# Attention weights of a graph layer: ScalarE bends seven of ten source tiles, VectorE multiplies them in one operation

## The chip, the core and the metric

The kernel runs on one core of a Trainium2 chip. The metric is the device time of one execution in microseconds (us); the core has TensorE (PE), VectorE (DVE), ScalarE (ACT), GpSimd (POOL) and the DMA queues, which run side by side and wait for each other through semaphores.

## What is computed

Two graph layers over 1250 nodes of 128 features and 20000 edges, each with a layer norm ahead of it and a residual sum behind it. The change lies in the first, an attention layer:

```
Wh = h @ W.T + b_W
s_s = Wh @ a_src
s_d = Wh @ a_dst
e = leaky_relu(s_s[src] + s_d[dst] + a_b[0], 0.2)
m = segment_max(e, dst);  ex = exp(e - m[dst])
denom = segment_sum(ex, dst)
h_prime = segment_sum((ex / denom[dst])[:, None] * Wh[src], dst)
```

A gated cell turns `h_prime` and `h` into new node states. The second layer does four steps of message passing by edge type, each with such a cell.

## The kernel before

The nodes are cut into ten tiles of 128. The attention isn't computed edge by edge. For each tile n of ten destination tiles the kernel counts how many edges run from each source node to each node of the tile, which gives ten blocks of 128 x 128 (one for each source tile i, source nodes on partitions). The weight of a block is this count times a function of the two scores, and because a leaky ReLU is the larger of two lines, that function is a product of exponentials up to one maximum: `max(fall[d], s_tall[s])`, where `fall` depends on the destination alone (a row, the same on all partitions) and `s_tall` on the source alone (a column). A further factor of the source, `s_gain`, is multiplied into `Wh` once. The matrix product of the weight blocks and `Wh` (with a column of ones for the denominator) then gives the attention sum of the tile.

The work of the ten tiles runs in turns J = 0 to 9, written out by hand for each engine (the functions `turn`), and staggered over them:

- VectorE in turn J makes the one-hot tiles of the turn's first half window (`one_hots`, into a ring of eight), unpacks the digits of tile J - 1 (`read_digits`), makes the weights of tile J - 2 (`weigh`), makes the one-hot tiles of the second half window, and takes the reciprocal of the denominator of tile J - 2 (`reciprocals`; that of tile 0 comes in turn 3 ahead of the digits).
- TensorE multiplies one-hot tiles (`window`, line 1441), turns the counts of tile J - 1 around into the other PSUM tensor (`count_turn`, line 1455), aggregates tile J - 2 with its weights (`aggregate`, line 1478), and multiplies the one-hot tiles of the second half.
- ScalarE evacuates the second half window of the turn before (`evac`, line 542), shifts the cell numbers of a coming window (`window_cells`, line 547), copies the attention row of tile J - 3 with its reciprocal (`attn_out`, line 582), evacuates the first half window, and brings the counts of tile J - 1 to SBUF (`counts_out`, line 554) and sums their excess (`excesses`, line 560). After turn 9 the calls for the last tiles are written out one by one, mixed with the first gates of the cell.

`weigh` is ten operations on VectorE per tile, line 965. It waits for the counts and, two tiles back, for the aggregation that frees its buffer; the weights go to two buffers in turn. The semaphore `probs` tells TensorE that they are done, and tells ScalarE that the counts may be overwritten.

Of the kernel before, what the change touches and what calls it, by code (L numbers as in the profile page):

```python
# [42 lines left out]
HOTS_BEFORE = (0, *accumulate(TILES))  # L43
AHEAD = 63
CELL_SETS = 4
SLOW = 5
LANE_PART = 20
WIN = 64
# [43 lines left out]
def build(nc, x, src, dst, attr, W, b_W, a_src, a_dst, a_b, res_W, res_b, Wi, Wh_g, bi, bh,  # L92
          W_edge, b_edge, W_ih, W_hh, b_ih, b_hh, out):
    with ExitStack() as ctx:
        def sb(name, shape, dt):
            return ctx.enter_context(nc.sbuf_tensor(name, shape, dt))
# [30 lines left out]
        def carve(shape, dt, size):  # L127
# [4 lines left out]
            if dt != BF16:  # L132
# [76 lines left out]
        s_peak = sb("s_peak", [P, 1], F32)  # L209
        s_back = sb("s_back", [P, 1], F32)  # L210
        s_tall = sb("s_tall", [P, NT], F32)
        s_low = sb("s_low", [P, 1], F32)
        s_flat = exp_b
        ab_col = sb("ab_col", [P, 1], F32)
# [68 lines left out]
                  "w_T w_sb bias_sb hn stats var rstd norm lanes "  # L283
                  "h_T h_sb b_cols proj_ps proj folded Wh_ps Wh s_ps s_rows d_ps s_dst s_peak s_up bent fallen s_fall s_gain gained")
        E1 = sems("e_", "sq link bound scale bias wide w_T w_sb spread rows_ps rows")
        K = sems("k_", "cellw pair slot evac digits countT absent counted excess rowmax logit "
                 "lmax shift exps probs probT probsb agg denom recip attn")
        G = sems("g_", "a_ps aS gates rz z uu vv n dd ee h turn")
        T = sems("t_", "ps full hi lo")
# [73 lines left out]
        def weights(n):  # L363
            return exp_b if isinstance(n, int) and n % 2 else exp_a
# [48 lines left out]
        def _(pool):  # L413
# [11 lines left out]
            g.iota(iota[:], pattern=[[1, CELLS]], base=0, channel_multiplier=0, **kw).then_inc(C.iota, 1)  # L425
            g.memset(zero16[:], 0.0).then_inc(C.const, 1)
            g.memset(power[:], -0.5).then_inc(C.const, 1)
            g.memset(few[:], 1.0 - BASE).then_inc(C.const, 1)
            g.memset(ones[:], 1.0).then_inc(C.const, 1)
            g.memset(Wh[:, :, P:P + 1], 1.0).then_inc(C.const, 1)  # L430
            for n, run in groupby(range(NS), lambda w: TILES[w]):
# [73 lines left out]
        def _(act):  # L505
# [74 lines left out]
            def attn_out(n, J):  # L580
                act.wait_ge(K.recip, n + 1)
                a.activation(attn[:, bass.ds(J, 1)].rearrange("p a d -> p (a d)"), psD[:, 0:P], ACT.Copy,
                             scale=denom_r[:, 0:1]).then_inc(K.attn, 1)

            def turn(J):
                if there(J - 1):
                    evac(J - 1, 1)
                    if 2 * J + 3 < NW:
                        window_cells(2 * J + 3)
                if there(J - 3):  # L590
                    attn_out(J - 3, J - 3)
                if J == 1:
                    falls()
                if there(J):
                    evac(J, 0)
                if 2 * J + 4 < NW:
                    window_cells(2 * J + 4)
                if there(J - 1):
                    counts_out(J - 1, count_sum[:, J - 1:J])
                    excesses(J - 1)  # L600

            def falls():
                act.wait_ge(S0.s_fall, 1)
                act.wait_ge(S0.d_ps, 1)
                a.activation(fall[:], smallf[:, 0:NP], ACT.Relu, bias=s_back[:, 0:1], scale=RISE).then_inc(S0.bent, 1)
                a.activation(s_tall[:], s_up[:], ACT.Exp, scale=RISE / SLOPE)
                act.wait_ge(S0.bent, 1)
                a.activation(fall[:], fall[:], ACT.Exp, scale=-1.0).then_inc(S0.fallen, 1)

# [46 lines left out]
            act.wait_ge(S0.s_ps, 1)  # L656
            a.activation(s_rows[:], smallf[:, 0:NP], ACT.Identity, bias=proj[:, 2:3]).then_inc(S0.s_rows, 1)
            turn(1)
            a.activation(s_gain[:], s_up[:], ACT.Exp).then_inc(S0.s_gain, 1)
            act.wait_ge(S0.s_gain, 1)  # L660
            for i in range(NT):
                last = a.activation(Wh[:, i], Wh[:, i], ACT.Copy, scale=s_gain[:, i:i + 1])
# [59 lines left out]


            evac(NT - 1, 1)
            attn_out(NT - 3, NT - 3)
            attention_in(0, 0)
            counts_out(NT - 1, count_sum[:, NT - 1:NT])
            attn_out(NT - 2, NT - 2)
            first_gates(0)
            excesses(NT - 1)  # L730
# [70 lines left out]
            with act.If(flag):  # L801
                act.sem_inc(K.probsb, NT)
                act.wait_ge(Z.weights, 1)
                a.activation(s_gain[:], s_up[:], ACT.Exp, scale=-1.0).then_inc(S0.s_gain, 1)
                act.wait_ge(S0.s_gain, 2)
                for i in range(NT):
                    last = a.activation(Wh[:, i], Wh[:, i], ACT.Copy, scale=s_gain[:, i:i + 1])
                last.then_inc(Z.plain, 1)
                a.activation(s_flat[:], s_rows[:], ACT.Copy, scale=SLOPE).then_inc(Z.flat, 1)
                with act.Fori(0, NT) as J:  # L810
                    slow_counts(J)
                    slow_absences(J)
                    counts_out(NT + J)
                    slow_exponentials(J)
                    probs_out(NT + J)
                    attn_out(NT + J, J)
                for c in range(NCH):
                    attention_in(NCH + c, c)
                    cell_gates(0, NCH + c, (NCH + c) % 2, c, CH)
                    cell_new(NCH + c, (NCH + c) % 2, CH)  # L820
                    second_norm(NCH + c, c)
                    second_h(NCH + c, c)
                with act.Fori(0, STEPS, 2) as s:
                    slow_step(s, 0)
                    slow_step(s + 1, 1)
# [6 lines left out]
        def _(dve):  # L832
# [125 lines left out]
            def weigh(n):  # L958
                dve.wait_ge(K.counted, n + 1)
                if n == 0:  # L960
                    dve.wait_ge(S0.fallen, 1)
                if n >= 2:
                    dve.wait_ge(K.agg, n - 1)
                for i in range(NT):
                    last = v.scalar_tensor_tensor(weights(n)[:, i * P:(i + 1) * P], fall[:, n * P:(n + 1) * P],  # L965
                                                  s_tall[:, i:i + 1], count[:, i * P:(i + 1) * P], ALU.max, ALU.mult)
                last.then_inc(K.probs, 1)

            def slow_row_max(J):
# [917 lines left out]
```

## Time and profile before

| what | us |
|---|---|
| median of 3 runs | 435.61 |
| lowest and highest | 435.06 and 438.87 |
| the profiled execution, its own time | 434.47 |
| its span, from the first to the last instruction | 432.3 |
| busy in the span: TensorE, VectorE, ScalarE, GpSimd | 370.1, 266.6, 150.8, 99.1 |

The span is what the trace covers, and the execution's own time has 2.17 us around it. Busy times of the engines overlap each other, so they don't add up to the span; an engine that is busy for a small part can still end the waits of another.

### The profile page before, as it was taken

To read this page: it belongs to the slowest core of one execution; us is meant where nothing else is said; L and a number is where in the kernel's file an instruction comes from. 1 tells how busy PE (TensorE), PEld (TensorE's weight loads), DVE (VectorE), ACT (ScalarE), POOL (GpSimd) and SP (SyncE) were. 2 spreads that over 40 slices of the span, in tenths; PEclk is the share of its full clock that TensorE was granted. 3 is DMA by queue.
4 is the path that set the end of the run, shared out by engine and by line. 5 is a ranking of instruction groups with operands and counts; after the bars stand their busy time and mean duration, and the time that the engine had idled before them with its cause. 6 is when DMAs were issued, how large, how long until landed. Compare 5 with 4: busy or idle time off the path is not lost.

```text
span 432.3 us, 6617 instructions
## 1 busy us (share of the span) xinstructions
PE 370.1 (86%) x2057; PEld 246.9 (57%) x2057; DVE 266.6 (62%) x797; ACT 150.8 (35%) x333; POOL 99.1 (23%) x136
## 2 busy tenths in 40 slices
PE   1459876777798888889899999999999999999993
PEld 0446543555556667644375674656655675747793
DVE  6997887688889765777365454436434545444144
ACT  3452266444445554443122222213122322312022
POOL 3102000000000000100177700577202775007300
PEclk9959996999999999999999999999999999999998
DMA  5200000000000000012213320233202242111200
GB/s 145 69 1 2 1 2 1 2 1 2 1 2 2 2 1 2 0 69 80 103 51 106 94 80 24 80 97 105 97 2 85 55 147 75 42 73 48 57 14 23
DMA packets 14498, 19.88 MB, mean 46 GB/s; under 512 B 2591, under 2 KB 7728, under 8 KB 14460
## 3 DMA queue, kind: packets, MB, share of 16 engines
q1 hardware_dynamic: 10276, 12.90, 8.4%
q0 software_dynamic: 2912, 5.97, 5.5%
q10 hardware_dynamic: 1272, 0.54, 0.5%
q8 instruction: 19, 0.31, 0.3%
q14 instruction: 19, 0.16, 0.1%
HBM read 8.27 MB, written 11.13 MB: 45 GB/s over the span
## 4 chain that ended last, share of the span: by engine, by line
PE 67%; DVE 19%; ACT 5%; issue 5%; DVEq 2%; DMA 0%; POOL 0%; SPq 0%; ACTq 0%; POOLq 0%
PE small L1590 27%; PE big L1572 7%; PE small L1478 6%; DVE scores L965 4%; DVE cell_hot L946 4%; PE big L1441 4%; PE small L1455 2%; PE small L1611 2%; DVEq L946 2%; PE small L1624 2%; PE big L1535 1%; PE small L1535 1%; PE small L1526 1%; PE small L1537 1%; PE small L1528 1%
## 5 line engine op out<-in xcount | busy, mean ns | idle before, releaser
L1590 PE MATMUL small<-nibbles,store 128*128 128x384 fp8e4 (+1 forms) x640 | 125.8, 353 | 1.3 <-DVE store L1118 0.8
L480 POOL DMA_INDIRECT scores<-messages,w_gat x91 | 87.7, 964 | 120.4 <-DMA messages<-store 93.9
L1590 PEld LDWEIGHTS small<-nibbles,store 128*128 128x128 f16 x640 | 62.3, 98 | 64.3 <-issue 7.2
L946 DVE TENSOR_SCALAR cell_hot<-iota,cell_w,fields 128x320 bf16<-128x320 f16 x231 | 65.7, 359 | 16.6 <-PE big L1441 15.6
L1441 PE MATMUL big<-cell_hot,store 128*128 128x320 bf16 x231 | 46.5, 324 | 14.0 <-DVE cell_hot L946 9.0
L721 ACT CAST store<-digit_words 128x512 f16<-128x512 f32 x40 | 24.6, 618 | 81.5 <-DVE digit_words L1114 81.5
L1114 DVE TENSOR_TENSOR digit_words<-big,edge_rows 128x512 f32<-128x512 f32 x40 | 27.4, 690 | 40.0 <-PE big L1572 39.9
L1441 PEld LDWEIGHTS big<-cell_hot,store 128*128 x231 | 31.3, 144 | 27.9 <-issue 25.6
L1572 PE MATMUL big<-wT,h 128*128 128x512 f32 x80 | 38.6, 599 | 2.3 <-ACT h L717 2.3
L1057 DVE SCALAR_TENSOR_TENSOR cell_hot<-rz,cell_hot 128x256 f32<-128x256 f32 (+2 forms) x29 | 11.0, 380 | 36.2 <-ACT cell_hot L692 36.2
L466 POOL TENSOR_TENSOR rstd<-var_e,power 128x2 f32<-128x2 f32 x5 | 3.5, 694 | 128.8 <-DVE var_e L1102 128.8
L1118 DVE TENSOR_TENSOR store<-digit_words,store 128x512 f16<-128x512 f32 x40 | 27.5, 689 | 6.1 <-ACT store L721 4.8
L691 ACT ACTIVATE rz<-small,gb 128x192 f32<-128x192 f32 (+1 forms) x14 | 6.2, 444 | 67.6 <-PE small L1537 67.6
L1455 PE MATMUL small<-nibbles,ident 128*128 128x512 fp8e4 (+1 forms) x120 | 25.3, 364 | 2.4 <-DVE nibbles L955 2.4
L965 DVE SCALAR_TENSOR_TENSOR scores<-scores,s_tall,tallies 128x128 f32<-128x128 f32 x100 | 27.2, 348 | 0.0
L1478 PE MATMUL small<-Wh,scores 128*128 128x129 f32 x200 | 24.8, 278 | 2.4 <-DVE scores L965 1.7
L1478 PEld LDWEIGHTS small<-Wh,scores 128*128 128x128 f32 x200 | 23.2, 191 | 5.1 <-DVE scores L965 3.4
L542 ACT CAST digit_words<-big 128x640 uint16<-128x640 f32 x20 | 13.8, 692 | 33.3 <-PE big L1441 18.1
L1230 DVE TENSOR_SCALAR aS<-small,edge_down 128x192 f32<-128x192 f32 (+2 forms) x24 | 9.7, 430 | 22.2 <-PE small L1590 17.3
L1572 PEld LDWEIGHTS big<-wT,h 128*128 128x128 f32 x80 | 14.5, 190 | 15.4 <-issue 10.6
L1455 PEld LDWEIGHTS small<-nibbles,ident 128*128 128x128 f16 x120 | 11.6, 102 | 15.8 <-DVE nibbles L955 4.5
L554 ACT ACTIVATE tallies<-small 128x1280 f32<-128x1280 f32 x10 | 12.4, 1238 | 19.9 <-DVE scores L965 10.7
(262 smaller groups left out, 493.2 us busy)
## 6 DMA issues: line engine op xcount, KB each, us to landing
messages<-store SPq DMA_DIRECT2D x40, 256.0 KB, 2.0
scores<-messages,w_gat POOLq DMA_INDIRECT x91, 2.5
xn<-in_x SPq DMA_DIRECT2D x1, 576.0 KB
out<-xn SPq DMA_DIRECT2D x4, 128.0 KB
store<-in_edge_attr SPq DMA_DIRECT2D x1, 256.0 KB
wn<-in_L_gnn_W_edge SPq DMA_DIRECT2D x1, 256.0 KB, 6.4
wn<-in_L_gnn_Wi ACTq DMA_DIRECT2D x1, 192.0 KB, 3.9
wn<-in_L_gnn_Wh_g ACTq DMA_DIRECT2D x1, 192.0 KB, 6.1
```

Source lines behind the costliest of these rows:

```text
L480: g.indirect_dma_start(out=rows16[:, u].rearrange("p a f -> p (a f)"), out_offset=None, in_=table_rows[s % 2][:], in_offset=bass.IndirectO ...
L542: a.copy(o.rearrange("p i (b d) -> p b i d", b=2), big[:, 2 * half:2 * half + 2, 0:HALF].rearrange("p b (i d) -> p b i d", d=SUB)).then_in ...
L721: a.copy(m16[s % 2][:, i, :, 0], full[:, i % 2].rearrange("p (t o) -> p t o", t=TYPES)).then_inc(T.hi, 1)
L946: last = v.tensor_scalar(half_hot[:, (before + q) % RING], iota[:, b * HALF:(b + 1) * HALF], cell_w[:, j % CELL_SETS, bass.ds(tile, 1)], f ...
L965: last = v.scalar_tensor_tensor(weights(n)[:, i * P:(i + 1) * P], fall[:, n * P:(n + 1) * P], s_tall[:, i:i + 1], count[:, i * P:(i + 1) * ...
L1114: v.tensor_tensor(full[:, i % 2], big[:, i % 2], edge_rows[:], ALU.add).then_inc(T.full, 1)
L1118: v.tensor_tensor(m16[s % 2][:, i, :, 1], full[:, i % 2].rearrange("p (t o) -> p t o", t=TYPES), m16[s % 2][:, i, :, 0], ALU.subtract).the ...
L1441: last = mm(big[:, 2 * half + b, 0:HALF], lane_hot[:, :, bass.ds(tile, 1)].rearrange("p l a -> p (l a)"), half_hot[:, (before + q) % RING] ...
L1455: last = mm(smallf[:, lo:hi], ident16[:], A8[:, q // 2, lo // P:hi // P, n * P:(n + 1) * P, q % 2], start=(q == 0), stop=(q == TYPES - 1), ...
L1478: last = mm(psD[:, 0:P + 1], w[:, i * P:(i + 1) * P], Wh[:, i], start=(i == 0), stop=(i == NT - 1), skip_group_check=True)
L1572: mm(big[:, i % 2], h1[:, i * P:(i + 1) * P], wT[:, W_EDGE:NWT].rearrange("p t o -> p (t o)"), start=True, stop=True).then_inc(T.ps, 1)
L1590: last = mm(bank[:, 0:w], m16[s % 2][:, i, t, part], A8[:, t % 2, i, lo:lo + w, t // 2], start=(i == 0 and part == 0 and t == 0), stop=(i ...
```

## The change

For source tiles 0 to 6 (`RAISED = 7`) the maximum goes to ScalarE. It holds the inverse of `s_tall` there and computes `raised = relu(fall * (1 / s_tall) - 1)`, one operation for each source tile, with a column of -1 as bias and the column of `s_tall` as scale. VectorE then makes the seven blocks with one operation 896 columns wide, `(raised + 1) * count`. The factor `s_tall` that was divided out is put into `s_gain` of these tiles, so both exponentials are now computed in two parts, 7 columns and 3. Source tiles 7 to 9 keep their three operations, which now come first. `raised` is one buffer, in memory that held the transposed weights of the other path, so ScalarE waits for the weights of the tile before until it overwrites it. GpSimd sets the column of -1 at the start. The core of the diff (left out are the declarations, the split of `s_gain` on the path that isn't taken here, and context):

```
+            def raises(n):
+                act.wait_ge(S0.fallen, 1)
+                if n >= 1:
+                    act.wait_ge(K.probs, n)
+                for i in range(RAISED):
+                    last = a.activation(raised[:, i * P:(i + 1) * P], fall[:, n * P:(n + 1) * P], ACT.Relu,
+                                        bias=below_one[:, 0:1], scale=s_tall[:, i:i + 1])
+                last.then_inc(K.raised, 1)
...
                 if there(J - 3):
                     attn_out(J - 3, J - 3)
+                if there(J - 2):
+                    raises(J - 2)
...
-                a.activation(s_tall[:], s_up[:], ACT.Exp, scale=RISE / SLOPE)
+                a.activation(s_tall[:, 0:RAISED], s_up[:, 0:RAISED], ACT.Exp, scale=-RISE / SLOPE)
+                a.activation(s_tall[:, RAISED:], s_up[:, RAISED:], ACT.Exp, scale=RISE / SLOPE)
...
-            a.activation(s_gain[:], s_up[:], ACT.Exp).then_inc(S0.s_gain, 1)
+            a.activation(s_gain[:, 0:RAISED], s_up[:, 0:RAISED], ACT.Exp, scale=1.0 / SLOPE)
+            a.activation(s_gain[:, RAISED:], s_up[:, RAISED:], ACT.Exp).then_inc(S0.s_gain, 1)
...
             evac(NT - 1, 1)
+            raises(NT - 2)
             attn_out(NT - 3, NT - 3)
             attention_in(0, 0)
             counts_out(NT - 1, count_sum[:, NT - 1:NT])
+            raises(NT - 1)
             attn_out(NT - 2, NT - 2)
...
-                for i in range(NT):
-                    last = v.scalar_tensor_tensor(weights(n)[:, i * P:(i + 1) * P], fall[:, n * P:(n + 1) * P],
-                                                  s_tall[:, i:i + 1], count[:, i * P:(i + 1) * P], ALU.max, ALU.mult)
+                for i in range(RAISED, NT):
+                    v.scalar_tensor_tensor(weights(n)[:, i * P:(i + 1) * P], fall[:, n * P:(n + 1) * P],
+                                           s_tall[:, i:i + 1], count[:, i * P:(i + 1) * P], ALU.max, ALU.mult)
+                dve.wait_ge(K.raised, n + 1)
+                last = v.scalar_tensor_tensor(weights(n)[:, 0:RAISED * P], raised[:, 0:RAISED * P], 1.0,
+                                              count[:, 0:RAISED * P], ALU.add, ALU.mult)
                 last.then_inc(K.probs, 1)
```

On ScalarE a middle turn (turn 5, say) read like this before, from the evacuation of the second half window of the turn before to the excesses; `digit_words` are the packed counts, `tallies` holds the counts and their excess:

```order
L542 CAST digit_words<-big 128x2x10x32 [waits k_digits,k_slot]
L547 ACTIVATE cell_w<-fields 128x160
L582 ACTIVATE attn<-small,denom_r 128x128 [waits k_recip]
L542 CAST digit_words<-big 128x2x10x32 [waits k_digits,k_slot]
L547 ACTIVATE cell_w<-fields 128x160
L554 ACTIVATE tallies,count_sum<-small 128x1280 [waits k_probs,k_countT]
L560 ACTIVATE tallies,excess_sum<-tallies,few 128x1280 [waits k_excess,k_counted]
```

In the changed kernel, whose line numbers are a little higher, the same turn reads so (`scores` is `fall`, and `raised` lies in `tallies`):

```order
L546 CAST digit_words<-big 128x2x10x32 [waits k_digits,k_slot]
L551 ACTIVATE cell_w<-fields 128x160
L586 ACTIVATE attn<-small,denom_r 128x128 [waits k_recip]
L594 ACTIVATE tallies<-scores,below_one,s_tall 128x128 [waits k_probs,s0_fallen]
L594 ACTIVATE tallies<-scores,below_one,s_tall 128x128 x6
L546 CAST digit_words<-big 128x2x10x32 [waits k_digits,k_slot]
L551 ACTIVATE cell_w<-fields 128x160
L558 ACTIVATE tallies,count_sum<-small 128x1280 [waits k_probs,k_countT]
L564 ACTIVATE tallies,excess_sum<-tallies,few 128x1280 [waits k_excess,k_counted]
```

Seven operations now stand between the attention copy and the evacuation of the first half window. On VectorE, the same turn before, from the unpacking of the digits to the first one-hot tile of the second half window:

```order
L954 TENSOR_SCALAR nibbles<-digit_words 128x10x128 [waits k_evac]
L955 TENSOR_SCALAR nibbles<-digit_words 128x10x128
L965 SCALAR_TENSOR_TENSOR scores<-scores,s_tall,tallies 128x128 [waits k_agg,k_counted]
L965 SCALAR_TENSOR_TENSOR scores<-scores,s_tall,tallies 128x128 x9
L946 REGISTER_ALU [waits k_slot,k_cellw]
...
L946 TENSOR_SCALAR cell_hot<-iota,cell_w,fields 128x320
```

And in the changed kernel:

```order
L974 TENSOR_SCALAR nibbles<-digit_words 128x10x128 [waits k_evac]
L975 TENSOR_SCALAR nibbles<-digit_words 128x10x128
L985 SCALAR_TENSOR_TENSOR scores<-scores,s_tall,tallies 128x128 [waits k_agg,k_counted]
L985 SCALAR_TENSOR_TENSOR scores<-scores,s_tall,tallies 128x128 x2
L988 SCALAR_TENSOR_TENSOR scores<-tallies 128x896 [waits k_raised]
L966 REGISTER_ALU [waits k_slot,k_cellw]
...
L966 TENSOR_SCALAR cell_hot<-iota,cell_w,fields 128x320
```

Ten operations without a wait among them became four, and the last of them waits for ScalarE's seven.

## Rows read from the trace of the kernel before

**Rows 1.** The page's chain that ended last, share of the span by engine

```profile
PE 67%; DVE 19%; ACT 5%; issue 5%; DVEq 2%; DMA 0%; POOL 0%; SPq 0%; ACTq 0%; POOLq 0%
```

**Rows 2.** Stretch, length, busy PE, PEld, DVE, ACT, POOL (count); granted clock; DMA

```profile
82.00:117.00 35.00, 27.30 (x171) 19.54 (x169) 28.99 (x105) 15.07 (x28) 0.00 (x0) 1.00 0.00 1
117.00:121.00 4.00, 3.81 (x12) 1.63 (x13) 4.00 (x16) 0.93 (x2) 0.00 (x0) 0.57 0.00 0
```

**Rows 3.** Groups of VectorE by form: shapes, count | busy us, mean ns | idle

```profile
L965 DVE SCALAR_TENSOR_TENSOR scores<-scores,s_tall,tallies 128x128 f32<-128x128 f32 x100 | 27.2, 348 | 0.0
...
L1118 DVE TENSOR_TENSOR store<-digit_words,store 128x512 f16<-128x512 f32 x6 | 4.0, 687 | 0.8 <-ACT store L721 0.7
...
L1076 DVE SCALAR_TENSOR_TENSOR h<-ee,cell_hot 128x256 f32<-128x256 f32 x5 | 2.1, 424 | 0.2
```

**Rows 4.** ScalarE's line 533 (Relu with bias and scale): ns min/median/max, first and last start

```profile
L533 ACT ACTIVATE hn<-xn,nmr,rstd x10: 490/492/503, 21.4 to 24.9; 128x128 f32<-128x128 f32 x10
```

**Rows 5.** Timeline of VectorE: start us, us, line, operation, count [idle before <-releaser]

```profile
72.28 2.71 DVE L965 SCALAR_TENSOR_TENSOR scores<-scores,s_tall,tallies 128x128 f32<-128x128 f32 x10
...
85.31 2.71 DVE L965 SCALAR_TENSOR_TENSOR scores<-scores,s_tall,tallies 128x128 f32<-128x128 f32 x10
...
106.69 2.72 DVE L965 SCALAR_TENSOR_TENSOR scores<-scores,s_tall,tallies 128x128 f32<-128x128 f32 x10
...
112.42 0.64 DVE L946 TENSOR_SCALAR cell_hot<-iota,cell_w,fields 128x320 bf16<-128x320 f16 x2 [1.10 <-PE big L1441]
...
127.05 2.71 DVE L965 SCALAR_TENSOR_TENSOR scores<-scores,s_tall,tallies 128x128 f32<-128x128 f32 x10
...
145.01 2.71 DVE L965 SCALAR_TENSOR_TENSOR scores<-scores,s_tall,tallies 128x128 f32<-128x128 f32 x10
...
152.53 2.71 DVE L965 SCALAR_TENSOR_TENSOR scores<-scores,s_tall,tallies 128x128 f32<-128x128 f32 x10
...
158.10 2.84 DVE L965 SCALAR_TENSOR_TENSOR scores<-scores,s_tall,tallies 128x128 f32<-128x128 f32 x10
```

**Rows 6.** Timeline of TensorE in the same stretch

```profile
75.99 1.28 PE L1441 MATMUL big<-cell_hot,store 128*128 128x320 bf16 x6 [0.94 <-DVE cell_hot L946]
...
88.08 2.50 PE L1478 MATMUL small<-Wh,scores 128*128 128x129 f32 x20 [0.28 <-DVE scores L965]
...
106.84 2.34 PE L1455 MATMUL small<-nibbles,ident 128*128 128x512 fp8e4 x12 [0.17 <-DVE nibbles L955]
109.47 2.50 PE L1478 MATMUL small<-Wh,scores 128*128 128x129 f32 x20 [0.28 <-DVE scores L965]
...
115.03 0.84 PE L1441 MATMUL big<-cell_hot,store 128*128 128x320 bf16 x4 [1.33 <-DVE cell_hot L946]
...
117.19 4.02 PE L1455 MATMUL small<-nibbles,ident 128*128 128x512 fp8e4 x12 [0.23 <-DVE nibbles L955]
...
155.30 2.49 PE L1478 MATMUL small<-Wh,scores 128*128 128x129 f32 x20
```

**Rows 7.** Timeline of ScalarE in the same stretch

```profile
64.31 0.19 ACT L659 ACTIVATE s_gain<-s_up 128x10 f32<-128x10 f32 x1
...
70.46 0.35 ACT L547 ACTIVATE cell_w<-fields 128x160 f32<-128x160 f32 x1
...
84.64 0.37 ACT L582 ACTIVATE attn<-small,denom_r 128x128 f32<-128x128 f32 x1 [3.39 <-DVE denom_r L998]
...
104.22 0.36 ACT L582 ACTIVATE attn<-small,denom_r 128x128 f32<-128x128 f32 x1
...
125.39 0.36 ACT L582 ACTIVATE attn<-small,denom_r 128x128 f32<-128x128 f32 x1
...
143.12 0.37 ACT L582 ACTIVATE attn<-small,denom_r 128x128 f32<-128x128 f32 x1
...
150.99 0.69 ACT L542 CAST digit_words<-big 128x640 uint16<-128x640 f32 x1 [0.36 <-PE big L1441]
...
155.50 1.24 ACT L554 ACTIVATE tallies<-small 128x1280 f32<-128x1280 f32 x1 [3.16 <-PE small L1455]
```

More of the change, by code:

```diff
@@ L45 @@
 CELL_SETS = 4
+RAISED = 7
 SLOW = 5
@@ L211, in build @@
         s_tall = sb("s_tall", [P, NT], F32)
+        below_one = sb("below_one", [P, 1], F32)
+        raised = probT
         s_low = sb("s_low", [P, 1], F32)
@@ L285, in build @@
         E1 = sems("e_", "sq link bound scale bias wide w_T w_sb spread rows_ps rows")
-        K = sems("k_", "cellw pair slot evac digits countT absent counted excess rowmax logit "
+        K = sems("k_", "raised cellw pair slot evac digits countT absent counted excess rowmax logit "
                  "lmax shift exps probs probT probsb agg denom recip attn")
@@ L427, in _ @@
             g.memset(power[:], -0.5).then_inc(C.const, 1)
-            g.memset(few[:], 1.0 - BASE).then_inc(C.const, 1)
+            g.memset(few[:], 1.0 - BASE)
+            g.memset(below_one[:], -1.0).then_inc(C.const, 1)
             g.memset(ones[:], 1.0).then_inc(C.const, 1)
@@ L803, in _ @@
                 act.wait_ge(Z.weights, 1)
-                a.activation(s_gain[:], s_up[:], ACT.Exp, scale=-1.0).then_inc(S0.s_gain, 1)
+                a.activation(s_gain[:, 0:RAISED], s_up[:, 0:RAISED], ACT.Exp, scale=-1.0 / SLOPE)
+                a.activation(s_gain[:, RAISED:], s_up[:, RAISED:], ACT.Exp, scale=-1.0).then_inc(S0.s_gain, 1)
                 act.wait_ge(S0.s_gain, 2)
```

## The prediction, made before the changed kernel ran

> **What bounds the kernel now.** I read the chain of work that ended last first, then the granted clock by stretch, then the timelines of the three busy engines side by side, turn by turn. The chain gives TensorE 67% of the span and VectorE 19% [rows 1], so VectorE does end things, but a share over the whole span doesn't say where. The change touches only the count stage, about 70 to 161 us [rows 5], turns of 9 to 11 us. There VectorE is busy 28.99 of 35 us and TensorE 27.30 [rows 2], so neither is simply full, and a share of busy time decides nothing; the hand-overs do.
>
> Take turn 5 [rows 5 and 6]. VectorE finishes the digit words and at 106.69 starts the ten weight operations, 2.72 us, to 109.41. TensorE got the same digits, and its transposing count begins at 106.84 and takes 2.34 us, to 109.18. The aggregation, which needs the weights, starts at 109.47 after 0.28 us of idle time that the weights ended. So the weights are the last thing TensorE waits for, but only just: the count ends 0.28 us before. After its weights VectorE makes the half hot tiles that fit its ring and then waits 1.10 us for TensorE (at 112.42 [rows 5]), whose next window stands behind the aggregation. This is what limits the change: time taken from the weights beyond 0.28 us becomes more of VectorE's wait.
>
> **VectorE's part.** Ten operations of 348 ns [rows 3] start (2.72 - 0.35) / 9 = 0.263 us apart. Three stay: 0.79 us. The new one is 896 wide, a form that isn't in the trace. The same operation with two immediates takes 424 ns at 256 columns, a two-tensor operation 687 ns at 512 [rows 3]: 1.03 ns a column, so 687 + 384 x 1.03 = 1.08 us. It can hardly be under 0.69 (the 512-wide one) nor over 1.48 (three and a half of the 256-wide one); I take 1.08. Weights of one tile: 0.79 + 1.08 = 1.87 us against 2.72, 0.85 us less, if the raised slices are there. Ten times that is 8.5 us of VectorE, which is not what the end gets.
>
> **ScalarE's part.** Each tile gets seven bent rows (Relu, 128 x 128, a column as bias and one as scale). The first layer norm uses just this form: 490 to 503 ns, ten starts from 21.4 to 24.9 [rows 4], 0.389 us apart. Seven take 6 x 0.389 + 0.49 = 2.83 us. Bounds: 3.52 without any overlap (7 x 0.503), and 1.95 if they ran like the attention copy, 0.37 us, which has a column only as scale [rows 7]. The row of the same form decides: 2.83, ten times 28 us on an engine with 15.07 of 35 us busy in this stage [rows 2]. They fit; the question is where they stand. In a turn they come behind the copy of the attention row three tiles back, which itself waits for VectorE's reciprocal, and ahead of the evacuation of the turn's first half, the counts and the excesses. The evacuation behind them waits for the same turn's digits anyway; its readers are a turn away; the counts wait for the weights' end. Those are hidden. The new wait is that of the wide operation for the raised slices, and behind it on VectorE stand the hot tiles of the turn's second half, on which TensorE's next window depends.
>
> **Turn by turn** (ScalarE's next operation starts 0.1 us before the one ahead ends, hand-over 0.04):
> - Turn 2: raising from 70.46 + 0.25 = 70.71 [rows 7] to 73.54, wide operation to 74.68, where the weights ended at 72.28 + 2.71 = 74.99 [rows 5]. TensorE waited 0.94 us for the hot tiles behind them (at 75.99 [rows 6]): gain 0.31.
> - Turn 3: here the reciprocal comes just ahead of the weights, so the attention copy runs at 84.64 [rows 7]; raising from 84.91 to 87.74, wide operation to 88.86 instead of 85.31 + 2.71 = 88.02 [rows 5]. The aggregation at 88.08 [rows 6] goes with it: loss 0.84.
> - Turns 4 and 5: attention copy at 104.22, raised by 107.32, three narrow operations until 106.69 + 0.79 = 107.48: no wait. Weights end at 108.56, and TensorE's count, to 109.18, is last. Gain 0.28 each.
> - Turn 6: the count takes 4.02 us, from 117.19 [rows 6], at a granted clock of 0.57 [rows 2]; the weights are hidden behind it. Gain 0.
> - Turns 7 to 9: the turn is shorter. Turn 7: copy at 125.39, raised at 128.48, end 129.60 against 127.05 + 2.71 = 129.76: gain 0.16. In turns 8 and 9 no cell operation stands ahead of the copy: 143.12, raised at 146.22, end 147.34 against 147.72 [rows 5 and 7], so the count is last again: 0.28 each.
> - Tail: raising of tile 8 begins behind the last evacuation, 150.99 + 0.59 = 151.58, to 154.41; wide operation to 155.53, and the aggregation of 155.30 [rows 6] is 0.2 late. It doesn't add up: tile 9 is raised behind the counts (155.50 + 1.24 [rows 7], so from about 156.8) until 159.63, so its weights end at 160.71, where they ended at 158.10 + 2.84 = 160.94 [rows 5]. I count a gain of 0.1, since the gates' own operations on ScalarE come later too.
> - Once: the gain exponential is split in two. It stands on the path ahead of the ten gain operations; one takes 0.19 us [rows 7]: loss 0.15. The split of the other exponential and the extra memset on GpSimd at the start lie beside other work: 0 (at most the same 0.2).
>
> Sum: -0.31 + 0.84 - 0.56 - 0.16 - 0.56 - 0.1 + 0.15 = -0.70 us. The profiled execution took 434.47 us (span 432.3 and 2.17 around it), which would be 433.8; it lies 1.14 below the median of the runs, 435.61, so I forecast 434.9. A measurement of this kernel tells about 1% (4.4 us) from no change, so this is no change.
>
> **Rivals.**
> 1. The wait on ScalarE takes the place of the work removed. Slices that don't overlap (3.52 us a tile) would come 0.69 us later: turn 2 loses 0.38, turn 3 1.53, turn 7 0.53, turns 8 and 9 0.3 each, the tail 0.6, turns 4 and 5 keep their 0.56 of gain; with the 0.15, +3.2, 438.8 us by the median. It decides from some 2.95 us a tile on, where the sum is zero. For it speaks that an operation costs ScalarE 0.389 us where it cost VectorE 0.263 [rows 3 and 4], against it that the row of the same form overlaps. The Trainium skill, "ScalarE: Activation LUTs" (Rules for kernel authors), says that relu, max and multiplication belong on VectorE and not on ScalarE; by that rule the move is a loss, and the two row prices agree with it per slice, but the rule doesn't see that seven slices become one operation on VectorE.
> 2. VectorE is the bound, as its share in this stage suggests: all of 0.85 us a tile would be gained, 8.5 us, 427.1. Against it: the 0.28 us and the 1.10 us of wait behind the weights [rows 5 and 6].
> 3. The clock. The slow count of turn 6 cost 4.02 - 2.34 = 1.68 us more; just ahead of it TensorE had waited 1.33 us for hot tiles (at 115.03 [rows 6]). Shifts of a few tenths may do away with it (then turn 6 gains its 0.28 too: 433.0) or bring another (436.6). The Trainium skill, "TensorE: Matmul & The Clock Gate" (What's actually happening), says that the slow clock is the resting state and that activity releases it; the trace agrees, with 0.57 (between the levels of 1.2 and 2.4 GHz) right behind that wait; but over the 35 us ahead of it the clock stayed at 1.00 with TensorE busy for 27.30 only [rows 2], so neither says which way it goes here.
>
> **How the numbers follow.** Forecast 0.60; rival 1 0.15, a third of it past +4.4 us, for which a tile must cost some 3.7 us (or the raising must hold something up that I hold for hidden); rival 2 0.05; rival 3 0.10 each way. So faster by over 1% 0.05, slower by over 1% 0.05, within 1% 0.90. The range, 432.6 to 438.0, takes in both ways of rival 3, the wide operation's two ends (0.4 us either way, mattering only in the four places where raising is last, 1.6 us) and most of rival 1; out stay rival 2 and the dear end of rival 1.
>
> **What would show it.** The ten weights shrink to about 1.9 us where VectorE doesn't wait, and the wide operation waits for ScalarE in turns 3, 7 and the tail, most in turn 3 (1.6 us). The aggregations start without idle time behind the count in turns 4, 5, 8 and 9. VectorE's wait for TensorE's window in turn 5 grows from 1.10 us to about 1.7. ScalarE's busy time rises by about 34 us as the page adds up single durations (70 x 0.49). The forecast is wrong if the aggregation's idle time in turn 5 stays 0.28 or grows, if slices start over 0.42 us apart, or if the count stage as a whole gets shorter by more than 3 us without a change in the clock.

## The result, and the profile after

The changed kernel takes 432.42 us (median of 8 runs, 431.23 to 432.90); the kernel before, measured beside it, took 435.75 (8 runs, 434.66 to 438.87). The ratio is 0.9913, with an interval of 0.989 to 0.9936, that is 2.8 to 4.8 us less. The change is clear of noise, where the prediction had called its -0.70 us no change; it stays within 1%, the case that the prediction held for the likeliest. The time lies 2.5 us under the predicted 434.9 and 0.2 under the range.

The page's chain of work that ended last, for the changed kernel:

```profile
PE 69%; DVE 15%; ACT 9%; issue 5%; DVEq 1%; DMA 0%; POOL 0%; SPq 0%; ACTq 0%; POOLq 0%
```

Beside [rows 1], VectorE has given up four points of the chain, and ScalarE has taken four. The same stretches as in [rows 2], with the same columns:

```profile
82.00:117.00 35.00, 27.42 (x181) 20.60 (x179) 26.05 (x86) 24.61 (x55) 0.00 (x0) 1.00 0.01 1
117.00:121.00 4.00, 3.77 (x26) 2.58 (x26) 3.99 (x13) 3.15 (x7) 0.00 (x0) 1.00 0.01 2
```

In 35 us VectorE is busy 26.05 us instead of 28.99, ScalarE 24.61 instead of 15.07, and TensorE about as long as before. The second stretch, where the granted clock stood at 0.57 (a mean that lies between the two levels, 1.2 and 2.4 GHz), is at 1.00 here; whether the change did that is a question for the experiments.

The new operations, grouped by line and form, of the count stage (count | busy us, mean ns | idle before and its releaser):

```profile
L594 ACT ACTIVATE tallies<-scores,below_one,s_tall 128x128 f32<-128x128 f32 x70 | 27.9, 485 | 0.0
L988 DVE SCALAR_TENSOR_TENSOR scores<-tallies 128x896 f32<-128x896 f32 x10 | 10.9, 1090 | 4.8 <-ACT tallies L594 4.8
L985 DVE SCALAR_TENSOR_TENSOR scores<-scores,s_tall,tallies 128x128 f32<-128x128 f32 x30 | 8.7, 345 | 0.0
```

The wide operation takes 1.09 us (1.08 had been worked out from [rows 3]); seven raised slices take 27.9 / 10 = 2.79 us (2.83 from [rows 4]). The wide operation waits 4.8 us in all for ScalarE. The timeline of VectorE says where:

```profile
88.89 1.09 DVE L988 SCALAR_TENSOR_TENSOR scores<-tallies 128x896 f32<-128x896 f32 x1 [1.54 <-ACT tallies L594]
...
107.96 0.87 DVE L985 SCALAR_TENSOR_TENSOR scores<-scores,s_tall,tallies 128x128 f32<-128x128 f32 x3
108.75 1.08 DVE L988 SCALAR_TENSOR_TENSOR scores<-tallies 128x896 f32<-128x896 f32 x1
...
113.13 0.64 DVE L966 TENSOR_SCALAR cell_hot<-iota,cell_w,fields 128x320 bf16<-128x320 f16 x2 [1.39 <-PE big L1464]
...
127.19 1.09 DVE L988 SCALAR_TENSOR_TENSOR scores<-tallies 128x896 f32<-128x896 f32 x1 [0.56 <-ACT tallies L594]
...
144.31 1.09 DVE L988 SCALAR_TENSOR_TENSOR scores<-tallies 128x896 f32<-128x896 f32 x1 [0.33 <-ACT tallies L594]
...
152.10 1.09 DVE L988 SCALAR_TENSOR_TENSOR scores<-tallies 128x896 f32<-128x896 f32 x1 [1.02 <-ACT tallies L594]
```

The longest wait, 1.54 us, is that of turn 3; the others are 0.38 us (turn 2), 0.56 (turns 7 and 8), 0.33 (turn 9) and, in the tail, 1.02 and 0.40. In turn 5 there is none: the weights of 106.69 to 109.41 in [rows 5] are here 107.96 to 109.83, 1.87 us. Now TensorE, in the timeline of the same stretch:

```profile
90.04 2.50 PE L1501 MATMUL small<-Wh,scores 128*128 128x129 f32 x20 [1.08 <-DVE scores L988]
...
108.10 2.34 PE L1478 MATMUL small<-nibbles,ident 128*128 128x512 fp8e4 x12 [0.18 <-DVE nibbles L975]
110.27 2.40 PE L1501 MATMUL small<-Wh,scores 128*128 128x129 f32 x20
...
115.48 0.80 PE L1464 MATMUL big<-cell_hot,store 128*128 128x320 bf16 x4 [1.08 <-ACT digit_words L546]
...
117.60 2.34 PE L1478 MATMUL small<-nibbles,ident 128*128 128x512 fp8e4 x12 [0.23 <-DVE nibbles L975]
```

L1478 is now the count and L1501 the aggregation. From the start of a count to the start of the aggregation behind it [rows 6] had 109.47 - 106.84 = 2.63 us, 2.34 of work and 0.28 of idle time. Here it is 110.27 - 108.10 = 2.17: less than the count itself is shown to take, and the aggregation is 0.10 shorter too. So the turn lost more than the idle time that it had. The reason stands in rows that I had not read, those of TensorE's weight loads (PEld). First the kernel before, turn 5:

```profile
106.84 2.06 PEld L1455 LDWEIGHTS small<-nibbles,ident 128*128 128x128 f16 x12 [0.40 <-DVE nibbles L955]
109.46 2.31 PEld L1478 LDWEIGHTS small<-Wh,scores 128*128 128x128 f32 x20 [0.56 <-DVE scores L965]
```

And the changed kernel, turn 5:

```profile
108.09 2.06 PEld L1478 LDWEIGHTS small<-nibbles,ident 128*128 128x128 f16 x12 [0.41 <-DVE nibbles L975]
110.17 2.31 PEld L1501 LDWEIGHTS small<-Wh,scores 128*128 128x128 f32 x20
```

The attention weights are the operand that the aggregation loads. Before, the last load of the count ended at 108.90, and the next stood waiting 0.56 us for the weights, while the count's last products ran beside it until 109.18. After, the first load of the aggregation follows at once (110.15 to 110.17), beside the count's last products. The Trainium skill, "TensorE: Matmul & The Clock Gate" (Step-by-step: what each phase is for), says this: a load of weights can be pulled ahead of matrix products in flight, so the next tile's weights load while this tile's products run. The trace agrees, with its load at 110.17 and products that are shown running until 110.44 (the profile models the ends of products).

The length of each turn, from the start of one count to the start of the next (the last row: to the start of the last aggregation), from the timelines of TensorE; for turn 5 it is 117.19 - 106.84 before and 117.60 - 108.10 after. "Before" is a second profile of the kernel before, because the first has the slow count in turn 6 (10.00 us there); the tail is taken from the first, because the second has a slow stretch there. All other turns of the two agree to 0.03 us.

| turn | before | after | forecast | measured |
|---|---|---|---|---|
| 2 | 13.00 | 12.63 | -0.31 | -0.37 |
| 3 | 10.94 | 11.59 | +0.84 | +0.65 |
| 4 | 10.46 | 9.89 | -0.28 | -0.57 |
| 5 | 10.35 | 9.50 | -0.28 | -0.85 |
| 6 | 8.86 | 8.31 | 0 | -0.55 |
| 7 | 9.10 | 8.67 | -0.16 | -0.43 |
| 8 | 8.86 | 8.68 | -0.28 | -0.18 |
| 9 | 7.98 | 7.56 | -0.28 | -0.42 |
| tail | 10.12 | 9.91 | -0.10 | -0.21 |
| sum | | | -0.85 | -2.93 |

With the split of the gain exponential (ten gain operations now start 66.11 - 65.79 = 0.32 us behind the first exponential instead of 0.22, so +0.10 for the 0.15 forecast) the turns make -2.83 us, for a forecast of -0.70.

Three of the turns, 3, 5 and 7, gained by something else besides: pauses of VectorE itself, in which it waits for no other engine that the profile shows, and which the changed kernel doesn't have. In the kernel before, behind the waits for TensorE of turns 5 and 7:

```profile
113.26 0.16 DVE L994 TENSOR_SCALAR denom<-small 128x1 f32<-128x1 f32 x1 [0.20 <-issue]
113.73 0.16 DVE L998 RECIPROCAL denom_r<-denom 128x1 f32<-128x1 f32 x1 [0.31 <-DVE denom L994]
114.06 2.27 DVE L946 TENSOR_SCALAR cell_hot<-iota,cell_w,fields 128x320 bf16<-128x320 f16 x8 [0.16 <-issue]
...
132.91 0.36 DVE L946 TENSOR_SCALAR cell_hot<-iota,cell_w,fields 128x320 bf16<-128x320 f16 x1 [0.20 <-PE big L1441]
133.43 2.00 DVE L946 TENSOR_SCALAR cell_hot<-iota,cell_w,fields 128x320 bf16<-128x320 f16 x7 [0.15 <-issue]
```

And the same operations in the changed kernel:

```profile
113.97 0.16 DVE L1017 TENSOR_SCALAR denom<-small 128x1 f32<-128x1 f32 x1 [0.20 <-issue]
114.16 0.16 DVE L1021 RECIPROCAL denom_r<-denom 128x1 f32<-128x1 f32 x1
114.46 2.28 DVE L966 TENSOR_SCALAR cell_hot<-iota,cell_w,fields 128x320 bf16<-128x320 f16 x8
...
131.44 2.27 DVE L966 TENSOR_SCALAR cell_hot<-iota,cell_w,fields 128x320 bf16<-128x320 f16 x8 [0.21 <-PE big L1464]
```

From `denom` to the first hot tile, turn 5 takes 114.06 - 113.26 = 0.80 us before and 114.46 - 113.97 = 0.49 after. In turn 7 the second hot tile starts 133.43 - 132.91 = 0.52 us behind the first before, where the eight after stand (2.27 - 0.36) / 7 = 0.27 apart. In turn 3 ten hot tiles in a row take 2.98 us before and 2.82 after. That is 0.31, 0.25 and 0.16 us. Time saved on the weights can't show here, since VectorE waits for TensorE just ahead (in turn 5 for 1.10 us before and 1.39 after). The pauses stand at these same operations in all four profiles here of kernels with ten weight operations (the kernel before twice, ScalarE's added work alone, and the kernel before with TensorE's wait filled), and in none of the nine of kernels with fewer. So they go with VectorE's part of the change and not with ScalarE's; what makes them stays open.

### The profile page after: what moved, and what is told of

Read it like the earlier page. It is cut to its first block, busy times and chain, and to the rows that moved or that the text cites. A ratio compares the mean times of both kernels' runs of the same rounds, so it can differ in the third digit from the quotient of the medians.

```text
span 430.3 us, 6639 instructions
## 1 busy us (share of the span) xinstructions
PE 369.6 (86%) x2057; PEld 247.5 (58%) x2057; DVE 258.5 (60%) x737; ACT 176.6 (41%) x405; POOL 98.6 (23%) x137
## 4 chain that ended last, share of the span: by engine, by line
PE 69%; DVE 15%; ACT 9%; issue 5%; DVEq 1%; DMA 0%; POOL 0%; SPq 0%; ACTq 0%; POOLq 0%
PE small L1613 27%; PE big L1595 7%; PE small L1501 5%; PE big L1464 5%; PE small L1478 3%; DVE cell_hot L966 3%; ACT tallies L594 3%; PE small L1634 2%; PE small L1647 2%; PE big L1558 1%; DVE scores L988 1%; PE small L1558 1%; PE small L1549 1%; PE small L1560 1%; DVE digit_words L1137 1%
## 5 line engine op out<-in xcount | busy, mean ns | idle before, releaser
L594 ACT ACTIVATE tallies<-scores,below_one,s_tall 128x128 f32<-128x128 f32 x70 | 27.9, 485 | 0.0
L1478 PE MATMUL small<-nibbles,ident 128*128 128x512 fp8e4 (+1 forms) x120 | 24.7, 357 | 2.1 <-DVE nibbles L975 2.1
L1501 PE MATMUL small<-Wh,scores 128*128 128x129 f32 x200 | 24.6, 277 | 2.0 <-DVE scores L988 1.1
L1501 PEld LDWEIGHTS small<-Wh,scores 128*128 128x128 f32 x200 | 23.2, 191 | 4.2 <-DVE scores L988 2.5
L1478 PEld LDWEIGHTS small<-nibbles,ident 128*128 128x128 f16 x120 | 11.3, 100 | 15.2 <-DVE nibbles L975 4.4
L718 ACT ACTIVATE cell_hot<-cell_hot 128x256 f32<-128x256 f32 (+2 forms) x29 | 11.1, 383 | 18.6 <-DVE cell_hot L1085 18.5
```

The costliest lines, as they stand in the source:

```text
L594: last = a.activation(raised[:, i * P:(i + 1) * P], fall[:, n * P:(n + 1) * P], ACT.Relu, bias=below_one[:, 0:1], scale=s_tall[:, i:i + 1])
L1478: last = mm(smallf[:, lo:hi], ident16[:], A8[:, q // 2, lo // P:hi // P, n * P:(n + 1) * P, q % 2], start=(q == 0), stop=(q == TYPES - 1), ...
L1501: last = mm(psD[:, 0:P + 1], w[:, i * P:(i + 1) * P], Wh[:, i], start=(i == 0), stop=(i == NT - 1), skip_group_check=True)
```

## The experiments

Theories. For the missing 2 us: the time to be had from earlier weights is 0.55 us a turn and not 0.28, because the aggregation's loads can start beside the count's last products; past that, the count is last (the bound by the count). Rival: VectorE itself is the bound, and all of its time saved would count. For the clock, theory A: the slow stretch falls where the phase of an execution puts it, in any kernel, and is no part of the gain. Theory B: it belongs to the kernel before, brought by TensorE's wait of 1.33 us for hot tiles just ahead, and its absence is part of the gain. The pauses have no experiment of their own. The diffs are against the changed kernel where nothing else is said.

**Both kernels once more, unchanged.**

> The kernel before once more, for a second trace of it. Theory A (the slow clock of turn 6 is a matter of one execution's phase): the granted clock of the count of turn 6 may be 1.00 here, and the slow count stands in another turn or is absent. Theory B (it is part of the kernel before, set by its waits): the same count takes about 4 us at about 0.57 again.

> The changed kernel once more. Theory A: a slow count of about 4 us may appear in some turn from 3 to 9. Theory B (the shorter waits of the changed kernel keep the clock): granted clock 1.00 from turn 3 to the tail again; time 431 to 433.

The kernel before took 436.91 us in its one run, and its turn 6 in the timeline of TensorE reads:

```profile
116.48 0.84 PE L1441 MATMUL big<-cell_hot,store 128*128 128x320 bf16 x4 [1.34 <-DVE cell_hot L946]
...
118.65 2.34 PE L1455 MATMUL small<-nibbles,ident 128*128 128x512 fp8e4 x12 [0.23 <-DVE nibbles L955]
```

The same wait stands ahead as in [rows 6], 1.34 us, and yet the count takes 2.34 us. Instead, the clock is low in the tail (stretch, length, busy times as in [rows 2], granted clock):

```profile
116.00:121.00 5.00, 4.02 (x20) 2.19 (x20) 5.00 (x19) 1.29 (x4) 0.00 (x0) 1.00 0.00 0
162.00:167.00 5.00, 4.83 (x23) 4.64 (x24) 0.11 (x1) 0.78 (x2) 0.00 (x0) 0.66 0.01 3
```

The changed kernel took 430.97 us in its one run, with the turns of its first profile to 0.03 us and a clock of 1.00 from turn 3 to the tail. So the wait alone doesn't bring the slow stretch: B as it stood fell. Turn 6 without it, 8.86 us, against 10.00 says that a slow count costs 1.14 us net, where rival 3 took 1.68 + 0.28.

**ScalarE's added work alone.** ScalarE raises as in the changed kernel, nobody uses it, and VectorE makes all ten blocks as before; the two exponentials are in one part each, as before. Two waits that the cut below leaves out keep the order: ScalarE waits for its own last raising, and VectorE, behind the stage, for all of them.

```diff
-                for i in range(RAISED, NT):
+                for i in range(NT):
...
-                dve.wait_ge(K.raised, n + 1)
-                last = v.scalar_tensor_tensor(weights(n)[:, 0:RAISED * P], raised[:, 0:RAISED * P], 1.0,
-                                              count[:, 0:RAISED * P], ALU.add, ALU.mult)
```

> ScalarE makes the seven bent rows of each tile, but nobody uses them; VectorE makes the weights as before with ten operations. It measures what the 28 us of added work on ScalarE cost by themselves. If they are hidden (my working): within 0.5 us of the kernel before, about 435.7. If the evacuation, counts or excesses behind them come late and hold up TensorE: 1 to 3 us slower.

435.65 us against 435.54, ratio 0.9992 (0.9973 to 1.0012), every turn as long as before to 0.02 us. In TensorE's timeline the idle time ahead of the aggregation is back:

```profile
98.27 2.34 PE L1474 MATMUL small<-nibbles,ident 128*128 128x512 fp8e4 x12 [0.35 <-DVE nibbles L973]
100.89 2.50 PE L1497 MATMUL small<-Wh,scores 128*128 128x129 f32 x20 [0.28 <-DVE scores L983]
```

28 us of work on ScalarE cost nothing that can be measured; what is left for them to cost in the changed kernel is VectorE's wait for them.

**VectorE's saving alone.** ScalarE raises tile 0 only, and every tile multiplies by that (the weights of the other tiles are left without their own maximum).

```diff
-                if there(J - 2):
-                    raises(J - 2)
+                if J == 2:
+                    raises(0)
...
-                dve.wait_ge(K.raised, n + 1)
+                dve.wait_ge(K.raised, 1)
```

> The bent rows are made for destination tile 0 only, and VectorE uses these for all ten tiles, so ScalarE's work and the wait for it are left out of nine tiles; the weights of those tiles are therefore other numbers. Theory 1 (TensorE's count is last behind the weights): turn 3 gains 0.4 instead of losing 0.8, turns 7 to 9 and the tail gain some 0.8 together, so about 2 us under the changed kernel, 430. Rival (VectorE is the bound): 8.5 us under the kernel before, 427.

430.33 us, ratio 0.9868 (0.9837 to 0.9899). TensorE's timeline, turns 3 and 4:

```profile
85.58 2.34 PE L1476 MATMUL small<-nibbles,ident 128*128 128x512 fp8e4 x12 [0.61 <-DVE nibbles L973]
87.76 2.40 PE L1499 MATMUL small<-Wh,scores 128*128 128x129 f32 x20
...
95.82 2.34 PE L1476 MATMUL small<-nibbles,ident 128*128 128x512 fp8e4 x12 [0.36 <-DVE nibbles L973]
97.99 2.40 PE L1499 MATMUL small<-Wh,scores 128*128 128x129 f32 x20
```

The two stand 2.18 and 2.17 us apart and the turns 3, 4 and 5 are 10.24, 9.89 and 9.50 us, 7 and 8 are 8.31: no profile here shows ones that are shorter by more than 0.01 us. The saving of 0.85 us a tile, ten times, would give 427; it didn't. This is the bound by the count.

**The raising ahead of the attention copy.** In turn 3 the raising waited behind a copy that waited for VectorE's reciprocal; here it goes first.

```diff
-                if there(J - 3):
-                    attn_out(J - 3, J - 3)
                 if there(J - 2):
                     raises(J - 2)
+                if there(J - 3):
+                    attn_out(J - 3, J - 3)
```

> The changed kernel with the seven bent rows ahead of the copy of the attention row in each turn, so that they no longer stand behind VectorE's reciprocal. If the loss of turn 3 comes from that order: its stretch from count to count falls from 11.6 us to some 10.3, turns 7 to 9 gain another 0.3 together, 1.5 us under the changed kernel, 430.9. If the wait is only ScalarE's speed: turn 3 stays at 11.6 us, the time at 432.4. If the later copy holds up the aggregation: slower than the changed kernel.

430.99 us, ratio 0.9885 (0.9846 to 0.9924). TensorE's timeline, turn 3 and the count of turn 4:

```profile
86.88 2.34 PE L1478 MATMUL small<-nibbles,ident 128*128 128x512 fp8e4 x12 [0.61 <-DVE nibbles L975]
89.05 2.40 PE L1501 MATMUL small<-Wh,scores 128*128 128x129 f32 x20
...
97.12 3.41 PE L1478 MATMUL small<-nibbles,ident 128*128 128x512 fp8e4 x12
```

Turn 3 goes from 11.59 to 10.24 us: the place in ScalarE's order cost 1.35 us there. In this profile a slow count (3.41 us) took 1.07 of it back in turn 4 (10.96 for 9.89). The turn shows the effect; the intervals of the two kernels' ratios overlap.

**Five slices and four slices.** The dividing line moved, so that ScalarE is done earlier and VectorE later.

```diff
-RAISED = 7
+RAISED = 5
```

> The changed kernel with five source tiles on ScalarE instead of seven: weights of 5 x 0.263 + 0.82 = 2.13 us on VectorE, raising of 2.05 us. Theory PEld (an aggregation gains 0.55 us, the whole wait of its first weight load, as soon as the weights end 0.57 us earlier; no more after that): every turn from 4 to 9 is 0.55 us shorter from count to count than before, turn 3 loses nothing, 2 us under the changed kernel, 430.4. Theory of the prediction (the gain ends at 0.28 us, the idle time of the matrix products): turns 0.28 shorter, about 432. If VectorE's time bounds the turn: slower than the changed kernel, since VectorE gets 0.26 us more work in each tile.

> Four source tiles on ScalarE: weights of 6 x 0.263 + 0.69 = 2.27 us, 0.45 less than before. Theory PEld (each tenth by which the weights end earlier is gained in full, up to 0.55 us): the turns from 4 to 6 are 0.45 us shorter from count to count than before (10.01, 9.90 and 8.41 us where the clock is full, the second with its own 0.3 us). Theory of the prediction (the end is at 0.28 us): 0.28 shorter.

Five: 430.75 us, ratio 0.9873 (0.9835 to 0.9911). Four: 431.03 us, ratio 0.9904 (0.9883 to 0.9924). Turn 4 with five, in TensorE's timeline:

```profile
95.64 2.34 PE L1478 MATMUL small<-nibbles,ident 128*128 128x512 fp8e4 x12 [0.36 <-DVE nibbles L975]
97.81 2.40 PE L1501 MATMUL small<-Wh,scores 128*128 128x129 f32 x20
105.53 2.34 PE L1478 MATMUL small<-nibbles,ident 128*128 128x512 fp8e4 x12 [0.18 <-DVE nibbles L975]
```

And with four:

```profile
95.76 2.34 PE L1478 MATMUL small<-nibbles,ident 128*128 128x512 fp8e4 x12 [0.36 <-DVE nibbles L975]
97.93 2.50 PE L1501 MATMUL small<-Wh,scores 128*128 128x129 f32 x20
105.76 2.34 PE L1478 MATMUL small<-nibbles,ident 128*128 128x512 fp8e4 x12 [0.23 <-DVE nibbles L975]
```

Both intervals overlap that of the changed kernel, so the medians don't rank the three; the turns do. With five the turn is 9.89 us, as short as with nothing raised at all in it; with four it is 10.00, so 0.11 of the 0.57 is not yet gained, and turns 7 and 8 are 8.40 and 8.41 for 8.31. The gain follows how much earlier the weights end until the load is no longer late, at some 0.55 us; with an end at 0.28 all three would have been alike.

**Filling TensorE's wait in the kernel before.** Theory B once more, from its other side: if TensorE's wait brings the slow stretch, filling the wait should take it away. Ten unused products stand ahead of the first half window in turns 4 to 6 of the kernel before.

```diff
                 if later(j, 2):
                     pe.wait_ge(K.evac, j - 1)
+                filler(2 * half, {8: 10, 10: 10, 12: 10}.get(j, 0))
```

> The kernel before with ten small matrix products (128 x 192, nobody reads them) ahead of the first half window in turns 4, 5 and 6, where TensorE waits 1.1 to 1.3 us for hot tiles. Theory B (TensorE's waits bring the slow count): fewer executions with a slow stretch, none at turns 4 to 7, the median 0.5 to 1 us lower. Theory A (only phase, no matter what TensorE does there): as the kernel before, 435.6, with the same spread of 4 us, or up to 0.5 us slower for the filling itself.

435.41 us, ratio 0.9995 (0.9971 to 1.0019), runs from 434.36 to 437.55: neither the median nor the spread moved, though its own profile has no slow count in turns 3 to 9. So filling the wait bought no time, and nothing here supports B; that such a wait plays a part in single executions isn't excluded.

**Filling the stretch ahead of turn 2 in the changed kernel.** The clock is low there in the profile of the changed kernel. Thirty unused products ahead of the edge weights.

```diff
                 if J == 1:
+                    pe.wait_ge(K.evac, 3)
+                    filler(0, 30)
                     edge_weights()
```

> The changed kernel with thirty such products ahead of the edge weights at the end of turn 1, where TensorE waits 3.6 us for ScalarE and then runs at half clock for some 6 us. If its idle time brings that slow stretch: granted clock 1.00 from 66 to 76 us and 1.5 to 2 us less, 430.5 to 431. If not, or if the products come in the way: within 0.5 us of the changed kernel, 432.4.

431.21 us, ratio 0.988 (0.9843 to 0.9918) against the kernel before. The stretch from 66 to 76 us, first of the changed kernel:

```profile
66.00:76.00 10.00, 6.40 (x25) 3.42 (x24) 6.19 (x19) 9.82 (x28) 0.20 (x1) 0.66 0.00 1
```

Then with the thirty products:

```profile
66.00:76.00 10.00, 8.06 (x60) 5.60 (x59) 6.32 (x20) 9.75 (x29) 0.20 (x1) 1.00 0.00 1
```

The clock is at 1.00 instead of 0.66 and the count there takes 2.34 instead of 2.89 us. The median is 1.2 us under that of the changed kernel in another comparison, less than the 1.5 to 2 expected, and the intervals overlap. Nor do the profiles show that the clock bought it: the last aggregation starts at 160.62 us with the products, and at 160.73 and 159.44 in the two profiles of the changed kernel, both with the low clock there. So the 1.2 us isn't shown to be the clock's, as the expectation of the last variant below takes it.

**Five slices and the raising first, without and with the thirty products.**

> Five source tiles on ScalarE, their rows ahead of the copy of the attention row. With five, ScalarE is last only in turn 3 (10.58 us from count to count, where 10.24 can be had) and a little in the tail; the order mends turn 3. Expected 0.3 us under the variant with five alone, 430.4; if the two edits mend different waits and add up fully, 429.3.

> The same with the thirty products that nobody reads ahead of the edge weights. They took 1.2 us off the changed kernel by keeping the clock at 1.00; if the two gains are independent: 1.2 us under the variant without them, 429.2. If the earlier start of the count stage is eaten by a slow stretch later: no gain, 430.4.

Without: 429.40 us, ratio 0.9869 (0.9849 to 0.9889). With: 429.08, ratio 0.9869 (0.9842 to 0.9895). The products add nothing that can be measured here. The wide operation of five slices takes 0.82 us, it waits for ScalarE in no turn, and but for turn 4, which has a slow count (3.21 us), its turns are those of VectorE's saving alone to 0.05 us, or shorter: 10.29, 9.52, three times 8.31, 7.43 (the tail is 9.32 us, 0.16 longer). These two are the best versions of the study: 1.3% under the kernel before, with intervals that end where that of the changed kernel begins (0.9889 and 0.9895 against 0.989). Their medians are 3.0 and 3.3 us under its median, from another comparison; by the ratios it is 0.44% of the kernel before, 1.9 us.

**The slow stretches.** Between turn 3 and the tail one stands in the first profile of the kernel before (turn 6), in the second (tail), in those of VectorE's saving alone, of five and of four slices (turn 6), and in those of the raising first and of five slices with the raising first (turn 4); none in the others. A turn with one is 0.9 to 1.3 us longer (10.76 for 9.89, 9.59 for 8.31). They come in kernels of either kind, at changing places; what sets them stays open.

## Why the prediction was wrong in size

- **What bounds the stage.** Right: the hand-over of the weights was the last wait, and VectorE, with the larger busy share, was not the bound (VectorE's saving alone gave 430.33, not 427).
- **The step that failed.** The prediction's limit was: "time taken from the weights beyond 0.28 us becomes more of VectorE's wait." The 0.28 us is the idle time of TensorE's products [rows 6]; what the weights held up was the load in front of them, 0.56 us. From the start of the count to the end of the aggregation it was 2.63 + 2.50 = 5.13 us and is 2.17 + 2.40 = 4.57. So the term of 0.28 us was mis-sized: it is 0.55 in turns 4 and 6 (turn 6 had been set at 0 for its slow count). Only 0.2 came this way in turns 7 and 8 and 0.4 in turn 9, where the wide operation waits for ScalarE (0.56, 0.56 and 0.33 us) and the weights aren't early enough for all of it. Four slices show that the gain is gradual. Of the 2.1 us between the forecast turns (-0.85) and the measured ones (-2.93), this term makes some 1.2: the turns 4 to 6 and 9, without the pause, and turn 6 at full clock.
- **A term put at nothing: VectorE's pauses.** The prediction took VectorE's other work over as it stood in the trace. Three pauses went, 0.16 us in turn 3, 0.31 in turn 5 and 0.25 in turn 7, some 0.7 of the 2.1 us. With them turn 5 comes out (0.55 + 0.31 for 0.85) and turn 7 (0.19 + 0.25 for 0.43). The 1.33 us that TensorE waited for hot tiles at the end of turn 5 [rows 6] became 1.08 this way. The profile names ScalarE's evacuation for the end of that wait, but in turn 7 the products start at 132.41 while the same evacuation runs until 132.65, and by the code TensorE's window waits for an earlier one.
- **The sentence holds with the right size.** VectorE's wait at 113.13 grew from 1.10 to 1.39 us, by the 0.85 - 0.55 that the load left over, and not to 1.7. So time saved beyond the load did become VectorE's wait.
- **Turn 3, where ScalarE's order costs.** Right in place, cause and size: VectorE's wait is 1.54 us (1.6 forecast), TensorE's idle time 1.08 (0.28 + 0.84 forecast), the turn 0.65 longer (0.84). From count to aggregation it is 3.42 - 2.63 = 0.79 longer, near the forecast; the pause that went takes 0.16 off. The raising first undid it.
- **Durations.** Right: 1.09 for 1.08 us, 2.79 for 2.83. The page's busy time of ScalarE rose by 25.8 us (150.8 to 176.6), not 34, since it counts operations that overlap once; the 70 durations of 485 ns do add up to 34.
- **Rival 1** (the slices don't overlap) fell: they start (2.79 - 0.485) / 6 = 0.38 us apart. The Trainium skill, "ScalarE: Activation LUTs" (Rules for kernel authors), would have relu and multiplication on VectorE. Per slice the prices agree with it (0.38 us on ScalarE, 0.263 on VectorE), but the move paid, because ScalarE's time is free in this stage (its added work alone: 0.9992) and seven slices on VectorE became one operation.
- **Rival 2** fell with VectorE's saving alone. **Rival 3** isn't shown: the slow count of turn 6 is gone in both profiles of the changed kernel, but it is gone in the second profile of the kernel before too, so its absence is no sign of the change.
- **What would show it.** The signs of being wrong that were named didn't come: the idle time in turn 5 went, the slices start 0.38 us apart, and the count stage is 2.93 us shorter and not over 3. VectorE waits for ScalarE in turns 2, 8 and 9 too; in turn 8 a cell operation does stand ahead of the attention copy (at 134.02 us before), other than the prediction says.
- The turns make -2.83 us and the medians -3.3 (435.75 to 432.42). The turns lie at the edge of the interval; whether the rest is chance or fewer slow stretches stays open.

## What to carry to other kernels

Price a late operand by the wait of the weight loads, not by the idle time of the matrix products: where a load can run beside the products ahead of it, an earlier operand gains more than that idle time, here 0.55 us a turn for 0.28. An engine's pauses in one trace needn't stay when its program changes; here 0.7 us of them went. When work moves to an idle engine, look at what stands ahead of it in that engine's order: here one copy that waited for a reciprocal took 1.35 us of the gain in a single turn. Then choose the split so that the receiving engine is done before it is waited for; five slices instead of seven, raised first, brought the ratio to the kernel before from 0.9913 to 0.9869.

## What was not expected of the hardware

The aggregation's products are 0.10 us shorter when their loads aren't late (2.40 for 2.50 us), and they start before the end that is shown for the products of the count (110.27 against 110.44; that end is modelled by the profile, so how far the two overlap isn't shown). VectorE pauses for 0.16 to 0.31 us at the same three places in every profile of a kernel with ten weight operations, and not at these in any other. Stretches of low granted clock (0.57 at 117 to 121 us in the first profile of the kernel before, 0.66 at 162 to 167 in the second) move between executions of the same kernel, with the same wait of 1.33 and 1.34 us at the place where one had it and the other had not.
